# First tile in four loads, later loads in another order, and the feed-forward matmul opened half by half, in a two-batch attention and LoRA kernel

## What is computed

```python
# x: (2, 1024, 2048)   ctx: (2, 2048, 2048)   W: (2048, 2048)
n = (x - mean(x)) / sqrt(var(x) + 1e-5)
x = x + fake_quant(n, s1, z1) @ fake_quant(ctx, s2, z2)
y = (x - mean(x)) / sqrt(var(x) + 1e-5)
A_eff = einsum('bn,nri->bri', gate, lora_A)        # 16 LoRAs, rank 32, 8 gates
B_eff = einsum('bn,nor->bor', gate, lora_B)
delta = (y @ A_eff.T) @ B_eff.T + (y @ lora_A_shared.T) @ lora_B_shared.T
x = x + y @ W + bias + delta
```

## Time and profile before

| | us |
|---|---|
| three runs | 1061.36, 1062.89, 1066.37 (median 1062.89) |
| the profiled execution, its own time | 1063.74 |
| its span, first to last instruction | 1061.7 |
| PE busy in it | 1003.1 (94%) |
| DVE busy | 532.3 (50%) |
| ACT busy | 311.5 (29%) |
| mean granted TensorE clock | 0.989 |

### The profile page before, as it was taken

How to read it: one execution, slowest core, us unless ns; L and a number is a source line. 1 busy time by engine, 2 the same in 40 slices (tenths; PEclk the granted TensorE clock), 3 DMA queues, 4 the chain that set the end, 5 groups by cost and what they waited for, 6 DMA issues and landing times.

```text
span 1061.7 us, 12294 instructions
## 1 busy us (share of the span) xinstructions
PE 1003.1 (94%) x4791; PEld 472.9 (45%) x4791; DVE 532.3 (50%) x764; ACT 311.5 (29%) x266; POOL 163.4 (15%) x199
## 2 busy tenths in 40 slices
PE   2778999799999999999999999999999999999996
PEld 1345444355544444444444444445544444444442
DVE  6754677879655455463423555987632023014010
ACT  4666731322032132232223743532121021003000
POOL 3101100101102211311510000020104004004110
PEclk9989999899999999999999999999999999999998
DMA  8869682767735446338599844456935025004010
GB/s 365 255 192 368 260 346 96 184 139 183 201 127 195 168 149 212 138 112 251 204 299 262 336 179 159 80 166 147 222 110 169 20 80 187 20 30 158 10 42 27
DMA packets 124392, 181.70 MB, mean 171 GB/s; under 512 B 96064, under 2 KB 96064, under 8 KB 111808
## 3 DMA queue, kind: packets, MB, share of 16 engines
q1 hardware_dynamic: 109600, 118.25, 37.3%
q0 software_dynamic: 13600, 58.73, 15.3%
q10 hardware_dynamic: 1152, 4.19, 1.0%
HBM read 128.72 MB, written 29.36 MB: 149 GB/s over the span
## 4 chain that ended last, share of the span: by engine, by line
PE 68%; DVE 11%; DMA 10%; issue 4%; ACT 3%; POOL 1%; SPq 1%; DVEq 0%; POOLq 0%; ACTq 0%
PE psum L1154 16%; PE psum L1156 16%; PE psum L1155 16%; PE psum L987 15%; DMA stage<-in_w 2%; DMA x<-in_x 2%; PE psum L1177 2%; DMA lhs<-in_lora_b 1%; DVE ring L1396 1%; DMA xn<-in_x 1%; DVE stats L1421 1%; DVE hl L1441 1%; DVE stats L1308 1%; DMA bias_sb<-in_bias 1%; DMA lhs<-ap_st 1%
## 5 line engine op out<-in xcount | busy, mean ns | idle before, releaser
L1154 PE MATMUL psum<-ring,lhs 128*128 128x512 f16 x1024 | 388.8, 380 | 9.4 <-DMA lhs<-hl 7.4
L1155 PE MATMUL psum<-ring,lhs 128*128 128x512 f16 x1024 | 388.8, 380 | 0.0
L1156 PE MATMUL psum<-ring,lhs 128*128 128x512 f16 x1024 | 388.8, 380 | 0.0
L987 PE MATMUL psum<-ring,lhs 128*128 128x512 bf16 x1024 | 235.2, 386 | 9.0 <-DMA lhs<-ap_st 7.1
L987 PEld LDWEIGHTS psum<-ring,lhs 128*128 128x128 bf16 x1024 | 101.4, 99 | 134.8 <-issue 15.4
L1154 PEld LDWEIGHTS psum<-ring,lhs 128*128 128x128 f16 x1024 | 100.3, 98 | 132.3 <-issue 10.1
L1156 PEld LDWEIGHTS psum<-ring,lhs 128*128 128x128 f16 x1024 | 100.4, 98 | 121.3 <-issue 0.8
L1155 PEld LDWEIGHTS psum<-ring,lhs 128*128 128x128 f16 x1024 | 100.3, 98 | 119.9 <-issue 0.8
L1448 DVE SCALAR_TENSOR_TENSOR x<-psum,sc,x 128x512 f32<-128x512 f32 (+1 forms) x64 | 45.3, 746 | 182.2 <-PE psum L1166 181.4
L748 ACT ACTIVATE ring<-stage,sc 128x2048 f16<-128x2048 f32 x32 | 63.7, 2002 | 202.6 <-PE psum L1156 159.4
L617 POOL TENSOR_TENSOR x<-x,bias_sb 128x512 f32<-128x512 f32 (+1 forms) x64 | 87.7, 1396 | 173.5 <-DVE xn L1431 98.2
(11 more groups left out here) (158 smaller groups left out, 644.9 us busy)
## 6 DMA issues: line engine op xcount, KB each, us to landing
stage<-in_w SPq DMA_DIRECT2D x38, 1024.0 KB, 6.0
stage<-in_ctx_in SPq DMA_DIRECT2D x30, 1024.0 KB, 7.9
out<-x POOLq DMA_DIRECT2D x64, 256.0 KB, 3.5
x<-in_x POOLq DMA_DIRECT2D x8, 1024.0 KB, 11.9
xn<-in_x POOLq DMA_DIRECT2D x8, 1024.0 KB, 7.3
x<-in_x POOLq DMA_DIRECT2D x4, 2048.0 KB, 15.9
lhs<-in_lora_a POOLq DMA_DIRECT2D x4, 1024.0 KB, 6.9
lhs<-in_lora_b SPq DMA_DIRECT2D x4, 1024.0 KB, 13.3
```

The source lines that it names most:

```text
L987: last = pe.matmul(psum[:, t, :], lhs_q[:, k, t * P:(t + 1) * P], ring_q[:, g, j % 2, u, :], start=(k == 0), stop=False)
L1154: pe.matmul(psum[:, t, :], hi, ring[:, g, 0, u, :], start=(kk == 0), stop=False)
L1155: pe.matmul(psum[:, t, :], hi, ring[:, g, 1, u, :], start=False, stop=False)
L1156: last = pe.matmul(psum[:, t, :], lo, ring[:, g, 0, u, :], start=False, stop=False)
```

## The change

Five things are changed. (1) Tile 0 of x is loaded in four parts of 512 columns by SP's queue, ahead of all else there, instead of in one by POOL's; each part has a semaphore, and DVE takes the statistics part by part, ahead of the identity and LoRA pattern. The parameters are loaded by ACT's queue. (2) LoRA A's first two parts are issued on POOL's queue right behind the tiles, and SP's loads of context groups 0 and 1 of block 1 behind the four turns. LoRA B's loads go ahead of context: the order is B0, B1, context group 2, B2, B3, context group 3, and the loads of block 2 wait for the last B product. (3) Tiles 4 and 5 are scaled by DVE ahead of some statistics and of the last group of the first block. (4) PE opens the feed-forward part with tile 0 alone, group 0, then tile 1's high half with it, group 1 of tile 0, and tile 1's low half, before going on in pairs from group 2. (5) On DVE W's group 0 is done ahead of tile 1's low half, and tile 2's statistics come after W's group 2 instead of ahead of tile 1's low half; ACT's root for tile 2 moves behind W's groups 2 and 3.

```diff
@@ SP's queue @@
-            sp.dma_start(pats_sb[:, 0:4 + NGATE], par).then_inc(par_in, 16)
+            for c in range(NBLK):
+                sp.dma_start(x2[:, 0, c * NW:(c + 1) * NW], x_tile[0, 0][:, c * NW:(c + 1) * NW]).then_inc(x0_in[c], 16)
...
             sp.wait_ge(x_in[1], 16)
             load_ctx(0, 0, [0, 1])
-            load_ctx(0, 1, [0, 1])
             for t in range(PT, TILES):
                 turn_q(t)
+            load_ctx(0, 1, [0, 1])
             sp.wait_ge(q_rows, SUMS)
...
             load_lora_b(0)
+            load_lora_b(1)
             load_ctx(0, 1, [2])
-            load_lora_b(1)
-            load_ctx(0, 1, [3])
             load_lora_b(2)
             load_lora_b(3)
+            load_ctx(0, 1, [3])
+            sp.wait_ge(be_full, 8)
             load_ctx(0, 2, [0, 1])
@@ POOL @@
-            load_x(range(4))
+            load_x(range(1, 4))
...
+            load_lora_a(0)
+            load_lora_a(1)
             root_pair(2)
-            load_lora_a(0)
             root_pair(3)
-            load_lora_a(1)
@@ ACT @@
+            act.dma_start(pats_sb[:, 0:4 + NGATE], par).then_inc(par_in, 16)
             act.wait_ge(consts, 1)
...
                 split_hi(b, 1)
+                w_groups(b, 0, [2, 3])
                 root(b, 1, 2)
-                w_groups(b, 0, [2, 3])
@@ PE, base0_pair @@
-                    for t in range(2):
-                        tile_in(t)
-                        bank_free(k, t)
-                    for g in range(NG):
+                    tile_in(0)
+                    bank_free(k, 0)
+                    pe.wait_ge(converted, grp_w(b, 0, 0) + 1)
+                    base_group(0, 0)
+                    high_in(1)
+                    bank_free(k, 1)
+                    high_group(1, 0)
+                    pe.wait_ge(converted, grp_w(b, 0, 1) + 1)
+                    base_group(0, 1)
+                    low_in(1)
+                    low_group(1, 0)
+                    base_group(1, 1)
+                    for g in range(2, NG):
                         pe.wait_ge(converted, grp_w(b, 0, g) + 1)
                         for t in range(2):
                             base_group(t, g)
@@ DVE, start @@
+            stats1(0)
+            variance([0])
             dve.wait_ge(pats, 2)
             dve.tensor_copy(ident_b[:, :], ident).then_inc(ident_ready, 1)
             lora_pattern()
-            stats1(0)
-            variance([0])
...
             round1(2)
+            round1(3)
             stats1(5, range(2))
-            round1(3)
             turn_out(2)
             stats1(5, range(2, NBLK))
+            variance([4, 5])
             head_group(2)
             turn_out(3)
-            variance([4, 5])
+            scale_rows([4, 5], 3)
             head_group(3)
-            stats1(6)
-            scale_rows([4, 5], 3)
+            stats1(6, range(2))
+            round1(4)
+            stats1(6, range(2, NBLK))
+            round1(5)
             stats1(7)
             variance([6, 7])
-            round1(4)
             scale_rows([6, 7], 4)
-            round1(5)
@@ DVE, ahead of the feed-forward part @@
                 evict1(b, j, 3)
-                early_stats2(b, 2)
-                late_stats2(b, 2)
+                w_group(b, 0, 0)
                 low2(b, 1)
                 evict1(b, j, 4)
                 evict1(b, j, 5)
-                w_group(b, 0, 0)
                 w_group(b, 0, 1)
                 evict1(b, j, 6)
                 evict1(b, j, 7)
                 w_group(b, 0, 2)
+                stats2(b, 2)
                 w_group(b, 0, 3)
```

More of the change, by code:

```diff
@@ L182, in build @@
         x_in = [sem(f"x_in{n}") for n in range(TILES)]
+        x0_in = [sem(f"x0_in{n}") for n in range(NBLK)]
         res_in = [sem(f"res_in{n}") for n in range(NBLK)]
@@ L1146, in last_bases, with high_group, low_group @@
                         base_group(t, g)
+            def high_group(t, g):
+                for u in range(GU):
+                    kk = g * GU + u
+                    hi = lhs[:, 0, kk, t * P:(t + 1) * P]
+                    pe.matmul(psum[:, t, :], hi, ring[:, g, 0, u, :], start=(kk == 0), stop=False)
+                    pe.matmul(psum[:, t, :], hi, ring[:, g, 1, u, :], start=False, stop=False)
+            def low_group(t, g):
+                for u in range(GU):
+                    lo = lhs[:, 1, g * GU + u, t * P:(t + 1) * P]
+                    pe.matmul(psum[:, t, :], lo, ring[:, g, 0, u, :], start=False, stop=False)
             def base_group(t, g):
@@ L1186, in _, with high_in, low_in @@
                 k = blk(b, 1, 0)
+                def high_in(t):
+                    pe.wait_ge(turned[0], turns2(b, t, 0))
+                def low_in(t):
+                    pe.wait_ge(turned[1], turns2(b, t, 1))
                 def tile_in(t):
-                    pe.wait_ge(turned[0], turns2(b, t, 0))
-                    pe.wait_ge(turned[1], turns2(b, t, 1))
+                    high_in(t)
+                    low_in(t)
                 def base0_pair():
-                    for t in range(2):
-                        tile_in(t)
-                        bank_free(k, t)
-                    for g in range(NG):
+                    tile_in(0)
[11 more added lines that the diff above has]
+                    for g in range(2, NG):
                         pe.wait_ge(converted, grp_w(b, 0, g) + 1)
@@ L1305, in stats1 @@
             def stats1(t, parts=range(NBLK)):
-                dve.wait_ge(x_in[t], 16)
+                if t:
+                    dve.wait_ge(x_in[t], 16)
                 for c in parts:
+                    if t == 0:
+                        dve.wait_ge(x0_in[c], 16)
                     last = dve.bn_stats(stats[:, t % 2, c, :], x2[:, t, c * NW:(c + 1) * NW])
```

2 lines of the change are left out of this document (1 added, 1 removed).

## The result

The changed kernel takes 1074.6 us (median of 4 runs, 1073.94 to 1075.98) against 1064.25 us of the kernel before in the same set: a ratio of 1.0101, interval 1.0072 to 1.013. The prediction was 1061.7, range 1052 to 1067, with 0.07 on slower by over 0.5%. It was wrong. The profiled execution took 1074.13 us, with a span of 1072.3 against 1061.7 before.

The account below looks back on a forecast made before the run. PE, busy 94% of the span, was taken to lose some 20 us in waits. Span 1061.7, less 4.2 up to block 1's column term, plus 1.3 and 1.7 for the openings, gave 1060.5; forecast time 1061.7, range 1052 to 1067.

Parts of the forecast that it names:

- Start, part 1: Start of the kernel: with tile 0 in four parts, PE's first work was to come 0.4 us earlier, between 0 and 2.
- Tile 4, LoRA A: Block 1, batch 0: PE's 7.05 us wait for tile 4 and 2.2 us behind it go; LoRA A 9.2 us ahead.
- rival (d): At the start, turns of tiles 4 and 5 stay at 10 us, slow by themselves; result near 1062; chance 0.05.
- LoRA B: Before block 1's column sum: PE's waits for LoRA B loads, 4.6 us, go; B ends at 95.9 instead of 109.6.
- Context group 3: Block 1: converted at 96.0, DVE's last copy at 107.65, so a new column sum wait of about 8 us; 4.2 left.
- Opening in batch 0: Feed-forward opening: PE's 6.20 us wait goes, but DVE's chain costs 1.3 us at the LoRA product (0 to 3.0).
- Opening in batch 1: Feed-forward opening: PE waits for tile 2's low half, cost 1.7 us (-1 to 2.8), swallowing 1.24 us saved.
- The sum: Whole kernel: 1061.7 - 4.2 + 1.3 + 1.7 = 1060.5 us of span, a forecast time of 1061.7.
- The rival on the slower side: Block 1's context group 3 lands at 98.9 or later, nothing gained there, openings cost 3.0; 1066.8 us; chance 0.12.

## Why the prediction was wrong

- **Start, part 1: the step that failed first.** "I count 0.4 us for PE's first work, between 0 and 2": it was 5.6 late, of the other sign. I reckoned only what DVE does with parts of a tile and never asked what a second queue and quarter rows do to the landing of the last part. The landing of tile 0's last part stands in no term of the sum; it came at 13.4, where DVE had the whole tile at 6.73 before. The one-load runs put PE's first work back at 15.5 to 16.3, still 0.5 to 1.3 behind the kernel before.
- **Tile 4, LoRA A: right, but for that shift.** Tile 4's matmuls at 55.49 without a wait (49.8 + 5.6 = 55.4), then 1.26 us at the column term (1.7), LoRA A at 72.46 (67.1 + 5.6 = 72.7). With one load it stands at 67.44. The first two turns took 4.24 us to issue instead of 10.74, so rival (d) is out. (The prediction's 46.7 for tile 4's arrival should read 46.1, 41.7 + 4.4; nothing hangs on it.)
- **LoRA B: nearly right.** One wait of 1.29 us was left where I had none; it was hidden behind the next one, the wait for the copies.
- **Context group 3: right.** Issued 87.27, converted 102.09, last copy ended 113.75; predicted 81.9, 96.0 and 107.65, each 5.4 to 6.1 late by the start. The new wait was 7.60 (about 8). The column term: 120.75 predicted, 126.08 measured, 120.80 with one load on SP's queue. The run with the context load ahead shows that 6 to 7 us were still to be had there.
- **Opening in batch 0: right in kind, too small.** Statistics behind group 2 were to cost 1.3 (0 to 3.0); 2.5 measured, of which the run with the old opening still has 0.7. Against the kernel before, and less the 1.2 of the start, group 3 was 1.7 late and not 1.3, DVE's first half of LoRA B, whose small loads queue behind the turns on SP, 2.3 (243.35 against 239.93), and the product 2.5. PE waited 3.27 us at W's group 2 (2.6 forecast), and 1.12 at 231.40, about where a wait for tile 2's halves was forecast; for that one the profile names no releaser.
- **Opening in batch 1: the second step that failed.** "DVE idles 2.7 us, about what it saves, and the rest goes as before": the idling was 2.96, but the rest did not go as before. Between group 0 and the next loads of W lie the low half, its turn and SP's queue, which I had followed in batch 0 (issue at 203.5, measured 204.75 less 1.17) and not in batch 1. On top, with the loads 0.9 us later, POOL's bias load gets ahead of them; taking that away gave 1.9 us back. W's group 3 was ready 5.4 us later (713.86 less 4.92, against 703.53) where 1.5 to 2.2 were forecast. Cost 5.7 instead of 1.7, outside its bounds of -1 to 2.8.
- **The sum.** The span came 11.8 us above the 1060.5: 5.4 at the column term (1.2 behind instead of 4.2 ahead), 1.2 in the opening of batch 0, 3.9 in that of batch 1, and 1.3 in the stretch between, for which the sum had no term.
- **The rival on the slower side** had the wrong place: it put the loss into a late context landing, worth 1066.8, and none of the cases had tile 0 late. The range therefore ended at 1067. With the start as forecast and the openings as measured the sum would be 1060.5 + 1.2 + 4.0 = 1065.7 of span; the run with one load had 1066.4.

## What to carry to other kernels

Before a load is cut up so that its first part comes sooner, ask when its *last* part comes: rows of 2 KB moved 0.48 MB in the first 3 us where rows of 8 KB moved 0.89 (4 KB: 0.80, and nothing was lost), and beside another queue with 8 KB rows they got half of the packets and so a fifth of the bytes. Where an instruction that waits is moved ahead of one that feeds a DMA queue, follow that queue to its next load, in each batch anew, and look at what other queues ask for in the same microsecond: a shift of 0.9 us let a 256 KB load ahead of two of 1 MB, and they landed 3 us slower. And work that is moved out of a busy stretch has to go into an idle one: in batch 0 the same four statistics came with 2.2 to 3.5 us behind W's group 2, and with 0.2 or nothing just ahead of it, where DVE stood still for 5.8.

## What I had not expected of the hardware

- Rows of 2 KB on SP's queue, almost alone: 0.48 MB in 3 us against 0.89 with rows of 8 KB, and nearly equal packet counts for two queues (230 and 224) with 1.70 and 0.42 MB. The same quarters on POOL's queue went in packets of 4 KB.
- A 256 KB load on POOL's queue, issued 0.5 to 0.8 us ahead of two 1 MB loads on SP's, went with a median landing of 8.9 to 9.3 us for these; held back, 6.1.
- Waits of much the same length lower the clock in one run and not in the next. The LoRA product of batch 0 was waited for 2.96 us in the run with tile 0 whole on POOL's queue, and the granted clock behind it was 0.72 (1.2 GHz for part of it, 2.4 else); with one load on SP's queue it was 2.99 and the clock stayed at 1.00. The windows of 274 to 282, in that order (the last three numbers are clock, DMA share, GB/s):

```profile
274.00:282.00 8.00, 5.04 (x22) 2.75 (x21) 3.77 (x6) 0.38 (x1) 0.00 (x0) 0.72 1.07 260
```

```profile
274.00:282.00 8.00, 5.01 (x40) 3.84 (x40) 2.67 (x7) 0.38 (x1) 0.00 (x0) 1.00 1.02 280
```

  From the first to the fifth of DVE's evictions of the first feed-forward block the lag against before grew from 0.21 to 3.05 in the first run and went from -1.14 to -1.50 in the second. It is one reason why runs of one kernel differ by 4 us and more, and why single spans are read by their parts here.
